# A post-norm decoder layer on one core: inputs of four stages loaded one stage ahead, and denominators inverted row by row inside the two attentions

## The reference

```python
x = _layernorm(x + _L0_attn_ref(x, ...))    # linear attention, 16 heads of 16, 128 random features
x = _layernorm(x + _L0_xattn_ref(x, ...))   # causal softmax attention over 154 memory keys and the tokens
x = _layernorm(x + _L0_ffn_ref(x, ...))     # 16 experts, 4 of them used by a token, and 2 shared ones
```

## Time and profile before

| | us |
|---|---|
| median of 3 runs | 2283.32 (2280.03 to 2288.05) |
| the profiled execution, its own time | 2282.77 |
| its span, first to last instruction | 2281.1 |
| TensorE busy | 1903.9 |
| VectorE busy | 1494.6 |
| ScalarE busy | 911.4 |
| GpSimd busy | 280.4 |

### The profile page before, as it was taken

The page is one execution under the profiler, slowest core; times in us unless marked ns, Lnnn a source line. Parts: engine busy times, 40 slices in busy tenths (PEclk is TensorE's granted clock), DMA queues, the critical chain, the costliest instruction groups (busy, mean ns, idle before and its releaser), DMA issues. The chain is left out here.

```text
span 2281.1 us, 41052 instructions
## 1 busy us (share of the span) xinstructions
PE 1903.9 (83%) x14336; PEld 1267.0 (56%) x14336; DVE 1494.6 (66%) x3231; ACT 911.4 (40%) x1398; POOL 280.4 (12%) x353
## 2 busy tenths in 40 slices
PE   7929899886488157998999999946679999999997
PEld 5617666665355023433444444314468888888886
DVE  7925444443598455876877888614298787777776
ACT  5605454443133004655655666641233223323322
POOL 2100000000232001111111111134240000000000
PEclk9959999998799557999999999978799999999999
DMA  6932322331588320221211221136610000000000
GB/s 182 212 102 86 99 99 93 103 99 71 147 230 202 96 85 12 74 67 49 79 62 61 74 67 50 37 110 216 188 51 29 5 24 29 28 1 28 20 10 10
DMA packets 172803, 187.44 MB, mean 82 GB/s; under 512 B 87617, under 2 KB 143825, under 8 KB 166481
## 3 DMA queue, kind: packets, MB, share of 16 engines
q1 hardware_dynamic: 157152, 171.12, 25.3%
q10 hardware_dynamic: 15472, 13.84, 2.4%
HBM read 114.33 MB, written 70.20 MB: 81 GB/s over the span
## 5 line engine op out<-in xcount | busy, mean ns | idle before, releaser
L1378 DVE TENSOR_REDUCE sa_piece_max<-sa_ps_m 128x1 f32<-128x512 f32 (+4 forms) x1024 | 486.3, 531 | 184.6 <-PE sa_ps_m L1220 124.0
L1335 ACT ACTIVATE sa_prob<-sa_ps_s 128x1024 f32<-128x1024 f32 (+3 forms) x480 | 374.9, 825 | 370.3 <-PE sa_ps_s L1247 216.1
L1215 PE MATMUL sa_ps_m<-sa_k,sa_q 96*128 96x358 bf16 (+7 forms) x1024 | 268.9, 304 | 5.2 <-DVE sa_piece_max L1378 2.2
L1715 DVE SCALAR_TENSOR_TENSOR mo_acc<-mo_ps_o,mo_keep,mo_acc 128x256 f32<-128x256 f32 x512 | 212.2, 476 | 71.7 <-PE mo_ps_o L149 71.6
L1581 ACT ACTIVATE mo_h_hi<-mo_h 128x512 fp32r<-128x512 f32 x144 | 91.0, 632 | 272.2 <-DVE mo_h L1697 272.2
L1354 POOL TENSOR_SCALAR_AFFINE_SELECT sa_prob<-sa_prob 128x256 f32<-128x256 f32 x256 | 102.5, 406 | 676.6 <-ACT sa_prob L1335 674.0
L1247 PE MATMUL sa_ps_s<-sa_q,sa_k 99*128 99x512 bf16 (+3 forms) x768 | 180.2, 330 | 2.1 <-ACT sa_prob L1335 2.0
L577 DVE TENSOR_TENSOR la_att<-la_ps_att,la_cap 128x512 f32<-128x512 f32 x128 | 88.5, 691 | 141.6 <-PE la_ps_att L492 141.6
L1213 PE MATMUL sa_ps_m<-sa_km,sa_q 96*128 96x154 bf16 x512 | 125.1, 246 | 66.8 <-DMA sa_vm<-mem 48.8
L1213 PEld LDWEIGHTS sa_ps_m<-sa_km,sa_q 96*128 96x128 bf16 x512 | 51.1, 100 | 224.1 <-issue 139.8
L537 ACT ACTIVATE la_phi_kT<-la_ps_kT 128x512 f32<-128x512 f32 x128 | 76.4, 597 | 246.2 <-PE la_ps_kT L473 246.2
(11 more groups left out here) (187 smaller groups left out, 3782.2 us busy)
## 6 DMA issues: line engine op xcount, KB each, us to landing
s_y<-la_y SPq DMA_DIRECT2D x16, 512.0 KB
s_x<-cl_xn SPq DMA_DIRECT2D x16, 512.0 KB, 6.2
s_y<-sa_y SPq DMA_DIRECT2D x16, 512.0 KB, 2.6
mw_raw<-experts SPq DMA_DIRECT2D x18, 384.0 KB, 3.5
s_q_parts<-pj_parts SPq DMA_DIRECT2D x16, 384.0 KB, 4.8
s_k_parts<-pj_parts SPq DMA_DIRECT2D x16, 384.0 KB, 2.6
la_q<-s_q_parts SPq DMA_DIRECT2D x16, 384.0 KB
la_k<-s_k_parts SPq DMA_DIRECT2D x16, 384.0 KB
```

The lines of the kernel that those rows point to most:

```text
L1215: last = nc.tensor.matmul(ps_m[:, s, a - lo:hi - lo], qs, k[g][0:STACK, j, a - MEM:hi - MEM], start=lo > 0, stop=True, skip_group_check=True)
L1335: nc.scalar.activation(dst, src, ACT.Exp, scale=HD ** -0.5).then_inc(expd[s], 1)
L1378: nc.vector.tensor_reduce(piece_max[:, j, t, n:n + 1], ps_m[:, s, 0:hi - lo], AX.X, ALU.max).then_inc(piece_done[s], 1)
L1715: last = nc.vector.scalar_tensor_tensor(acc[:, t], ps_o[:, s, t], keep[:, n * TB + t, i - 1:i], acc[:, t], ALU.mult, ALU.add)
```

## The change

1. Input tiles, and the semaphores on which they land, now belong to objects that live across two phases (`LinearInputs`, `SoftmaxInputs`, `CloseInputs`). Two of four linear slots are loaded by SP's queue during project, after the second and the third batch row; two of four softmax slots the same way during close 1. The constants and the first row's two halves for close 1 are loaded during the last row of the linear attention, those for close 2 during the last row of the softmax attention.
2. The denominators of a batch row are loaded, inverted and stored inside the attention for rows 0 to 2, and only those of row 3 in the close phase. SP's queue does it at the end of a row; VectorE waits for them in the middle of the next row's first quad (linear), or after 40 of 64 reductions for the next row's second quad (softmax).
3. In project, close 1 (SP) and both attentions (VectorE) loops over batch rows are written out. GpSimd in the close phases first waits for SP's start.

```diff
@@ project, SP
-            with sp.Fori(0, B) as b:
+            for b in range(B):
                 batch_row(b)
+                if 1 <= b <= linear.EARLY:
...
+                    linear.load(sp, io, 0, b - 1)
@@ linear_attention, SP
             def around(kk, more):
                 for pr in range(SLOTS):
                     sp.wait_ge(y_done[pr], kk * BLOCKS + BLOCKS + START)
                     sp.dma_start(io["y"][...], y[:, pr]).then_inc(stored[pr], 16)
                     if more:
-                        load(kk + 1, pr)
-
-            for pr in range(SLOTS):
-                load(0, pr)
+                        linear.load(sp, io, kk + 1, pr)
+                    elif pr == 0:
+                        sp.wait_ge(inv_out, 16 + START)
+                        closing.load_consts(sp, io)
+                        for half in range(HALVES):
+                            closing.load(sp, io, 0, half)
+                if more:
+                    for pr in range(SLOTS):
+                        sp.wait_ge(stored[pr], kk * 16 + 16 + START)
+                    sp.dma_start(den[:, :], den_rows(io, kk)).then_inc(den_in, 16)
+                    sp.wait_ge(den_inv, kk + 1 + START)
+                    sp.dma_start(inv_rows(io, kk), den[:, :]).then_inc(inv_out, 16)
+
+            for pr in range(linear.EARLY, SLOTS):
+                linear.load(sp, io, 0, pr)
@@ linear_attention, VectorE
                     for c in range(BLOCKS):
+                        if kk and pr == 0 and c == BLOCKS // 2:
+                            dve.wait_ge(den_in, kk * 16 + START)
+                            chain.link(nc.vector.tensor_scalar(den[:, :], den[:, :], DEN_EPS * FEAT, None, ALU.add))
+                            if kk > 1:
+                                dve.wait_ge(inv_out, (kk - 1) * 16 + START)
+                            nc.vector.reciprocal(den[:, :], den[:, :]).then_inc(den_inv, 1)
@@ close_attention, SP
-                sp.dma_start(inv[:, 0, a], heads.unsqueeze(1).broadcast_to([HEADS // CT, HD, TILE])).then_inc(first_in, 16)
...
+            sp.dma_start(den[:, :], den_rows(io, B - 1)).then_inc(den_in, 16)
...
+                if on and 1 <= b <= softmax.EARLY:
...
+                    softmax.load(sp, io, 0, b - 1)
@@ softmax_attention, SP: at a row's end, as in the linear attention
+                if not last:
+                    for pr in range(2):
+                        sp.wait_ge(stored[pr], b * (QUADS // 2 * 16) + QUADS // 2 * 16 + START)
+                    sp.dma_start(den[:, :], den_rows(io, b)).then_inc(den_in, 16)
+                    sp.wait_ge(den_inv, b + 1 + START)
+                    sp.dma_start(inv_rows(io, b), den[:, :]).then_inc(inv_out, 16)
+
+            for g in range(softmax.EARLY, QUADS):
+                sp.wait_ge(cleared, g + 2 + START)
+                softmax.load(sp, io, 0, g)
@@ softmax_attention, VectorE, DEN_AT = 40
+                if b and g == 1:
+                    reduce_pieces(b, g, FIRST_PIECES, DEN_AT)
+                    dve.wait_ge(den_in, b * 16 + START)
...
+                    nc.vector.reciprocal(den[:, :], den[:, :]).then_inc(den_inv, 1)
```

More of the change, by code:

```diff
@@ L81, in __exit__, with begun, close @@
             self.nc.all_engine_barrier()
+    def begun(self, eng):
+        eng.wait_ge(self.held[-1], START)
+    def close(self):
+        self.ctx.close()
     def sb(self, name, shape, dt=F32):
-        return self.ctx.enter_context(self.nc.sbuf_tensor(f"{self.name}_{name}", shape, dt))
+        return self.ctx.enter_context(self.nc.sbuf_tensor(f"{self.name}_{name}", shape, dt, side=self.side))
     def ps(self, name, shape, dt=F32):
@@ L393, in linear_attention @@
         ident = ph.sb("ident", [P, P])
-        q = [ph.sb(f"q{i}", [STACK1, 4, T], BF16) for i in range(SLOTS)]
-        k = [ph.sb(f"k{i}", [STACK1, 4, T], BF16) for i in range(SLOTS)]
-        v = [ph.sb(f"v{i}", [P, BLOCKS, VW]) for i in range(SLOTS)]
+        q, k, v, landed = linear.q, linear.k, linear.v, linear.landed
+        den = ph.sb("den", [P, P])
         phi_kT = ph.sb("phi_kT", [P, 2, 4, P])
@@ L569, in _ @@
             dve.wait_ge(consts_in, 16 * N_CONST + START)
-            with dve.Fori(0, ROUNDS) as kk:
+            chain = Chain(dve, chain_sem)
+            for kk in range(ROUNDS):
                 for pr in range(SLOTS):
@@ L677, in use @@
             return b * (HALVES * NS // 2) + half * (NS // 2) + s // 2
[L679 to L692, removed]
         def load_inputs(eng, b, half):
             eng.wait_ge(biased, tile(b, half) + 1 + START)
-            load_y(eng, b + 1, half)
-            load_inv(eng, b + 1, half)
-            load_x(eng, b + 1, half)
+            closing.load(eng, io, b + 1, half)
         @blk.sync
@@ L754, in batch_row @@
                                      v[:, half, t].rearrange("p (g h) d -> p g (h d)", g=QUADS)).then_inc(v_out[half], 16)
[L756 to L758 removed]
+            for b in range(B):
+                batch_row(b, b + 1 < B)
+                if on and 1 <= b <= softmax.EARLY:
+                    for s in range(NS):
+                        sp.wait_ge(qk_out[s], 16 * HALVES + START)
+                    for half in range(HALVES):
+                        sp.wait_ge(v_out[half], 16 * TB + START)
+                    softmax.load(sp, io, 0, b - 1)
             for half in range(HALVES):
@@ L1180, in batch_row @@
                     if not last:
-                        load(b + 1, g)
-            for g in range(QUADS):
-                sp.wait_ge(cleared, g + 1 + (g > 0) + START)
-                load(0, g)
+                        softmax.load(sp, io, b + 1, g)
+                    elif g == 1:
+                        sp.wait_ge(inv_out, 16 + START)
+                        closing.load_consts(sp, io)
+                        for half in range(HALVES):
+                            closing.load(sp, io, 0, half)
+                if not last:
[7 more added lines that the diff above has]
+                softmax.load(sp, io, 0, g)
             maxima(0, 0)
@@ L1404, in _ @@
             reduce_pieces(0, 0, 0, FIRST_PIECES)
-            with dve.Fori(0, B - 1) as b:
+            for b in range(B):
                 chain.restart()
@@ L1408, in _ @@
                     quad(b, g)
-            chain.restart()
-            for g in range(QUADS):
-                quad(B - 1, g)
 EXPERT_W = 2 * C + C
```

231 lines of the change are left out of this document (144 added, 87 removed).

## The result

The changed kernel takes 2357.65 us, the median of 4 runs (2355.64 to 2361.94). The kernel before, with a fourth run beside its three, has a median of 2284.81. The ratio to it is 1.0319, interval 1.0300 to 1.0337: slower by 3.2%. The forecast was 2345, in a range of 2285 to 2385.

A forecast was written before the change was run, and what follows sets the result against it. It took slot loads on a few DMA engines to bound the linear attention and DMA to bound project and close 1; 38 + 42 - 27 + 26 - 38 + 30 - 8.5 = +62.5 on 2282.8 gave 2345 us, range 2285 to 2385.

The forecast's parts named there:

- Part 1: Project: two early linear slots put 49.6 us on two engines, little of it hidden; +38 us.
- the two bounds: Project's lengthening: 39 us at least with idle engine time judged by bytes, 48 by the DMA share of 0.96.
- Part 2: Linear attention: denominators land behind slot loads, VectorE waits for them and rows' rounds take 118 us against 100; +42 us.
- Part 3: Close 1's head: constants and first halves are already there, only row 3's denominators remain; -27 us.
- Part 4: Close 1's tiles: each of two early softmax slots pushes about 13 us through; +26 us, ends 0 and 50.
- Part 5: Softmax attention's start: with two slots present, the first maxima are issued at about 823, not 861.78; -38 us.
- Part 6: Softmax attention's rows: VectorE waits for denominators loaded behind the next slot; +30 us for three rows, 0 to 45.
- Part 7: Close 2's head: `yn` starts right behind GpSimd's remainders, at 1523 instead of 1530.24; -8.5 us.
- Moved loads are hidden: Rival: early slots find idle engine time in project and close 1, denominator waits remain; 2291 us, chance 0.17.
- The denominators aren't held back: Rival: the small denominator load overtakes the slot's, so both attentions' waits for it fall away; 2238 us, chance 0.09.
- Everything is hidden: Rival: early loads cost nothing and compute bounds the linear attention; -128 us, 2155 us, chance 0.04.
- Nothing is hidden: Rival: project +48, close 1 +50, and a fuller ring delays the linear attention further; 2385 us, chance 0.08.

The follow-up runs named there:

- e1: Changed kernel with one DMA for each copy of a part in place of broadcast DMAs, spreading slot loads over all engines; 2181.44 us, 0.9554 of before.
- e3: Changed kernel with the load of a row's denominators issued ahead of the fourth slot's load in both attentions; 2282.01 us, 0.9992 of before.
- e8: Changed kernel with close 1's two early softmax slots issued on ScalarE's queue in place of SP's; 2369.13 us, 1.0375 of before.
- e5: Changed kernel with no softmax slot loaded during close 1, all four at the softmax attention's start; 2354.91 us, 1.0309 of before.
- e10: Changed kernel with one DMA per copy, denominators ahead of the fourth slot, two linear slots early, no softmax slot early; 2149.35 us, 0.9400 of before.
- e2: Kernel before with one DMA for each copy of a part in its slot loads in place of broadcast DMAs; 2191.14 us, 0.9596 of before.
- e7: Changed kernel with one DMA for each copy of a part and no slot loaded early, linear or softmax; 2169.79 us, 0.9494 of before.

## Why the prediction was right

**Part 1, project: right, at +42.4 for 38.** Two slots x 24.8 less the idle time; it measured between the two bounds (39 and 48) and not at the 38 taken, which lay below its own lower bound. e1 shows the other side of the same sum: with all engines carrying the slots, 13.4.

**Part 2, linear attention: mechanism right, size 10.7 too high.** First denominators at SP's start + 153.2 (157.7 forecast), rounds of 115.3 and 115.5 us (118), tail 75.3 (76), VectorE's waits 40.4, 20.1 and 27.6 (45, 25, 25). The round had 29.5 us for its first slot, a duration read where the engines had been idle and the constants came ahead. In the second round the four slots and the denominators took 102.6 us, from the first issue at 337.21 to 439.84, where the sum had 105.7. The larger part of the miss, 4.5, lies ahead of the first denominators. That these were there at 324.57, for 324 forecast, is luck: project ended 4.4 later than forecast, and the six loads took 4.5 less. e3 confirms that the denominators waited for the slot ahead of them, with its 2.3 us from issue to landing.

The Trainium skill ("DMA: Bandwidth & Descriptors", section "Queues, rings and completion order") says that each engine takes a ring's descriptors in turn, and that SP and ScalarE have one ring each on the same sixteen engines, not engines of their own. The trace agrees in both: the denominators' 21 us behind the slot, and e8's 25.48.

**Part 3, close 1's head: right**, -26.6 for -27.

**Part 4, close 1's tiles: mis-sized**, +45.2 for +26. The step that failed is "the parts' buffers hold about half a tile's delay, so each of two loads pushes about 13 us through". A load pushes 22.6. Of the 25 us that I gave a slot only 2.4 were hidden, not 12. SP itself stands in the issue of the slot's last DMAs (15.32 and 14.53 us), so that for 35.5 us, the time of two tiles, no store is issued at all, and ScalarE then waits 30.4 for one. I had weighed only the engines' time and not that SP can't issue meanwhile. But e8 takes the slot off SP's queue and gets nothing back, so SP's standing alone isn't the cause: stores held by the slot, and ScalarE standing in SP's place, cost as much. How they share the loss is open. The end of my range, 50, was nearer. e5 measures the term by itself: 44.4.

**Part 5, softmax head: right**, -38.9 for -38. The maxima are issued at SP's free moment, 915.33, 68.2 behind the first memset in place of 107.0. **Part 6: right**, +31.4 for +30, the waits 28.9 in all. **Part 7: right**, -10.4 for -8.5.

The terms' errors cancel in part: +4.4, -10.7, +0.4, +19.2, -0.9, +1.4, -1.9, and -1.5 for the rest, give the 10.4 by which the sum was low. That the total is this near owes something to luck: without the 10.7 too many in part 2 it would have been 21 low.

**The rivals.** *Moved loads are hidden* falls in both stages (42.4 and 45.2). *The denominators aren't held back* falls by the waits; e3 shows how near it was: one slot less ahead of them, and the kernel ties with before. Its price was also badly worked out: I gave it -8 in the linear attention, where e3 with waits of 47 us left measures -11 already (418.0 for 429.4). *Everything is hidden* falls by the same stages. e1 and e10 (2181 and 2149) come near its 2155 by another way: even with spread loads project is 13 us longer in both, and what they gain comes from slots that pass in half the time. *Nothing is hidden* had 48 and 50 us for project and close 1; they measured 42.4 and 45.2, so it was nearer there than the forecast in close 1, but its further delay in the linear attention didn't come. What this kernel lacked was not time to hide the loads in but engines to carry them.

## What to carry to other kernels

Before moving a transfer ahead, divide its bytes by the bandwidth of its own window and look at the DMA share beside it: 0.25 with nothing else running says that a few engines carry it, and then it costs nearly its full length wherever stores need those engines (here 42.4 and 45.2 us for two slots of 25). Here rewriting the broadcast as one DMA for each 16 partitions was worth more (4%) than all the moving, which made the kernel 3% slower without it. With it, the change as it stands came out 0.4% under the spread kernel before, with intervals that overlap (e1, e2), 1% under it with no slot early (e7), and 2% only with the denominators ahead and no softmax slot early (e10).

A small load that someone waits for goes ahead of large ones on the queue, or its consumer waits for all of them; one place in the order was 75.6 us here.

## What the hardware showed that I hadn't expected

Spreading a slot, from a DMA share of a quarter to a full one, raised the rate from 77 to 151 GB/s only, while the share went from 0.25 to 1.07: an engine's busy time for the same bytes doubled. In close 1's tiles sixteen engines moved 233 GB/s at 0.87. Why the slot's reads pass so much slower when all engines carry them isn't settled by these runs. Two candidates weren't tried: the copies of one part read the same 128 KB, and each of the new DMAs writes only 16 of the 128 partitions.

Four stores on SP's queue were held 25 us while a slot was loaded by ScalarE's (e8), so here a second queue was no way around engines that were busy.
